# One VectorE operation for causal mask and row minimum of negated scores; gate columns beside the values; a new order of work

## The reference, cut to what matters

```python
h = _layernorm(x, axis=-1) * (1 + ca) + sa                 # ca, sa: one row per batch
# attention on h: RMS norm, then 16 heads of 64
sim = einsum('bhid,bhjd->bhij', q, k) * SCALE
sim = where(causal_mask, -finfo.max, sim)                  # mask above the diagonal
attn = softmax(sim, axis=-1)
out = einsum('bhij,bhjd->bhid', attn, v)
gates = sigmoid(x @ Wg)                                    # one gate per token and head
out = (gates * out) @ Wout
x = x + ga * out
h = _layernorm(x, axis=-1) * (1 + cb) + sb
# feed forward on h: silu(h Wg + bg) * (h Wu + bu) @ Wd + bd, plus experts:
sim = einsum('btphn,hkpn->pbthk', q, keys)                 # 2 x 4 heads x 64 keys
sc, ix = top_k(sim, 8)                                     # per half; then the best 8 of the 64 sums
x = x + gb * (mlp + experts)
```

## Time and profile before

| | us |
|---|---|
| median of three runs | 1555.74 (1555.52 to 1555.81) |
| the profiled execution, its own time | 1555.38 |
| its span in the trace | 1553.6 |
| PE busy | 1480.7 |
| DVE busy | 1347.4 |
| ACT busy | 1142.6 |
| POOL busy | 1098.7 |

### The profile page before, as it was taken

The page is one execution under the profiler, slowest core; times in us unless marked ns, Lnnn a source line. Parts: engine busy times, 40 slices in busy tenths (PEclk is TensorE's granted clock), DMA queues, the critical chain, the costliest instruction groups (busy, mean ns, idle before and its releaser), DMA issues.

```text
span 1553.6 us, 39532 instructions
## 1 busy us (share of the span) xinstructions
PE 1480.7 (95%) x12385; PEld 1194.9 (77%) x12385; DVE 1347.4 (87%) x3993; ACT 1142.6 (74%) x3687; POOL 1098.7 (71%) x1203
## 2 busy tenths in 40 slices
PE   4899999999999999999999999999999999999963
PEld 2577888787888878788887878888787888878753
DVE  4579998989999998999999899999989999998874
ACT  2677777887777788777778877777887777788731
POOL 2027787777778777777877777787777778777677
PEclk7899999999999999999999999999999999999976
DMA  4000000000000000000000000000000000000000
GB/s 126 18 14 18 14 23 22 22 17 15 20 14 22 22 22 15 17 18 16 22 22 22 15 17 17 17 22 22 22 15 17 16 18 22 22 22 8 12 12 9
DMA packets 46126, 32.01 MB, mean 21 GB/s; under 512 B 5680, under 2 KB 41328, under 8 KB 45968
## 3 DMA queue, kind: packets, MB, share of 16 engines
q1 hardware_dynamic: 45856, 31.20, 7.2%
q10 hardware_dynamic: 240, 0.43, 0.1%
HBM read 27.31 MB, written 4.31 MB: 20 GB/s over the span
## 4 chain that ended last, share of the span: by engine, by line
PE 90%; DVE 5%; POOL 2%; ACT 2%; issue 1%; DMA 0%; POOLq 0%; ACTq 0%; DVEq 0%
PE pS L1029 11%; PE pW L964 11%; PE pW L965 10%; PE pW L966 10%; PE pW L1045 9%; PE pS L1018 7%; PE pS L1014 7%; PE pW L1069 6%; PE pW L1105 4%; PE pW L1108 4%; PE pS L1020 3%; PE pW L1049 3%; PE pS L1021 2%; PE pW L1097 2%; POOL fexp L421 1%; PE pW L978 1%
## 5 line engine op out<-in xcount | busy, mean ns | idle before, releaser
L529 ACT ACTIVATE pS<-pS,nmx 128x128 f32<-128x128 f32 (+1 forms) x1024 | 390.4, 426 | 33.5 <-DVE nmx L728 30.9
L421 POOL TENSOR_TENSOR fexp<-fexp,fsum 128x512 f32<-128x512 f32 x256 | 342.1, 1373 | 64.9 <-DVE fexp L864 64.9
L745 DVE TENSOR_TENSOR p_sb<-pS,coef 128x256 f32<-128x256 f32 (+1 forms) x512 | 261.7, 552 | 8.9
L412 POOL TENSOR_TENSOR fsum<-ex 128x512 f32<-128x512 f32 x256 | 258.3, 1047 | 0.0
L521 ACT COPY pT<-pS 128x768 f32<-128x768 f32 x256 | 212.5, 848 | 19.5 <-PE pS L1029 19.5
L1029 PE MATMUL pS<-ident,p_sb 128*128 128x128 f32 x1536 | 217.4, 278 | 8.5 <-DVE p_sb L745 8.4
L1029 PEld LDWEIGHTS pS<-ident,p_sb 128*128 128x128 f32 x1536 | 171.4, 141 | 28.5 <-issue 16.3
L864 DVE TENSOR_SCALAR fexp<-fsum,top,rz 128x512 f32<-128x512 f32 x256 | 192.1, 813 | 1.2
L727 DVE TENSOR_REDUCE nmx<-pS 128x2 f32<-128x256 f32 x256 | 108.3, 423 | 91.2 <-PE pS L1021 84.9
L529 ACT ACTIVATION_READ_ACCUMULATOR pS<-pS,nmx 128x1 f32 x1024 | 185.7, 181 | 0.0
L728 DVE TENSOR_REDUCE nmx<-pS 128x2 f32<-128x512 f32 x256 | 174.1, 680 | 0.0
(11 more groups left out here) (178 smaller groups left out, 3923.1 us busy)
## 6 DMA issues: line engine op xcount, KB each, us to landing
modB<-mods_dram SPq DMA_DIRECT2D x32, 256.0 KB, 3.2
x_in<-in_L_attn_tokens SPq DMA_DIRECT2D x32, 128.0 KB, 2.1
modA<-mods_dram SPq DMA_DIRECT2D x32, 128.0 KB, 3.1
x_res<-in_L_attn_tokens SPq DMA_DIRECT2D x32, 128.0 KB, 3.0
out<-yo SPq DMA_DIRECT2D x32, 128.0 KB, 1.9
modC<-mods_dram SPq DMA_DIRECT2D x32, 64.0 KB, 3.1
fsum<-in_L_attn_Wkv SPq DMA_DIRECT2D x1, 1024.0 KB, 6.7
fsum<-in_L_attn_Wq SPq DMA_DIRECT2D x1, 512.0 KB, 4.9
```

The source lines that it names most:

```text
L412: ins = nc.gpsimd.tensor_tensor(fsum[:, k, h], ex[:, k, h, 0:NX].unsqueeze(2).broadcast_to([P, NX, NK]), ex[:, k, RH + h, :].unsqueeze(1). ...
L421: ins = nc.gpsimd.tensor_tensor(fexp[:, k, h, :], fexp[:, k, h, :], fsum[:, k, h].rearrange("p i j -> p (i j)"), ALU.mult)
L529: ins = nc.scalar.activation(ps, ps, ACT.Exp, bias=nmx[:, p % 2, h, k:k + 1], accum_out=den(p)[:, h, k:k + 1])
L745: ins = nc.vector.tensor_tensor(p_sb[:, p % 2, :, cols_of(k)], pS[:, p % 2, :, cols_of(k)], coef[:, :, k:k + 1].broadcast_to([P, 2, (k + 1 ...
```

## The change

In `scores`, the four mask products go, and with them the bfloat16 identity and mask. In `row_max`, the two reductions become four `tensor_tensor_reduce` operations, one per head and token block: each adds a float32 mask from SBUF to the scores in PSUM, negates, writes the result back in place and accumulates the row's minimum, which an accumulator read behind each operation writes to `nmx`. The exponential gets the factor -1. A `nop` (`apart`) stands ahead of the four.

The 16 gate columns stand ahead of the values of the first four heads; a token block's values now come in three pieces (272, 384 and 384 columns) in place of two of 512 and the gate projection. ACT takes the tanh of the gates from the first piece.

The scale and shift of the second LayerNorm move from DVE to ACT, where they are one operation on the transposed rows (`modulate_h`), with scale and shift loaded as two columns (`col`, a new DMA per batch; the load `modB` shrinks from 256 to 128 KB). The eight largest similarities are found in `shift`, straight from PSUM, before the exponential; `sim_tops` and the reductions of L832 go, one subtraction (`top_d`) and one exponential on ACT (into `tops`) come. `finish` handles both token blocks at once. On POOL, `add_heads(0)` and `fold(0)` stand ahead of `weigh(1)`. The lists of calls of all engines are written in another order.

```diff
+GV = 2 * DI
+VCUT = (0, 4, 10, H)
+NV = len(VCUT) - 1
...
+LARGEST = 3e38
...
-        ident_bf = sb("ident_bf", [P, P], BF16)
-        mask = sb("mask", [P, P], BF16)
+        mask = sb("mask", [P, TB * P])
...
                 weigh(0)
+                add_heads(0)
+                fold(0)
+                rstd2()
                 weigh(1)
-                add_heads(0)
-                rstd2()
                 rstd1()
-                fold(0)
+                add_heads(1)
                 rms1()
-                add_heads(1)
                 fold(1)
                 if isinstance(i, int) and i == -1:
                     split_weights()
...
-                                ins = nc.scalar.activation(ps, ps, ACT.Exp, bias=nmx[:, p % 2, h, k:k + 1], accum_out=den(p)[:, h, k:k + 1])
+                                ins = nc.scalar.activation(ps, ps, ACT.Exp, bias=nmx[:, p % 2, h, k:k + 1], scale=-1.0, accum_out=den(p)[:, h, k:k + 1])
...
-                        k, half = divmod(n, 2)
-                        evacuate(v[:, k, half * BANK:(half + 1) * BANK], w.bank("V", n)[:, :], "V", n)
+                        k, c = divmod(n, NV)
+                        heads = slice(VCUT[c] * DH, VCUT[c + 1] * DH)
+                        w.wait_full("V", n)
+                        bank = w.bank("V", n)
+                        first = 0
+                        if c == 0:
+                            first = H
+                            if k == 0 and w.live(-1):
+                                act.wait_ge(S(coef_ready), at(coef_ready, i - 1, 1))
+                            nc.scalar.activation(g_th[:, k, :], bank[:, 0:H], ACT.Tanh, scale=0.5)
+                        w.release(nc.scalar.copy(v[:, k, heads], bank[:, first:first + heads.stop - heads.start]), "V", n)
...
-                                             ACT.Exp).then_inc(S(ex_ready), 1)
+                                             ACT.Exp)
+                        if k == TB - 1:
+                            act.wait_ge(S(top_d_ready), at(top_d_ready, f, 1))
+                            if w.live(-2):
+                                act.wait_ge(S(cand_ready), at(cand_ready, g, 1))
+                            nc.scalar.activation(tops[:, :, :, :].rearrange("p a h n -> p (a h n)"), top_d[:, :, :, :].rearrange("p a h n -> p (a h n)"),
+                                                 ACT.Exp).then_inc(S(tops_ready), 1)
...
+                def modulate_h():
+                    if w.has("hT"):
+                        w.wait_full("hT")
+                        act.wait_ge(S(col_loaded), at(col_loaded, f, 16))
+                        o = w.bank("hT")[:, 0:N]
+                        nc.scalar.activation(o, o, ACT.Identity, bias=col[:, 0:1], scale=col[:, 1:2]).then_inc(S(h2T_mod), 1)
...
-                        nc.vector.reduce_max(nmx[:, s % 2, :, 0], pS[:, s % 2, :, 0:P], AX_X, negate=True)
-                        nc.vector.reduce_max(nmx[:, s % 2, :, 1], pS[:, s % 2, :, P:SW], AX_X, negate=True).then_inc(S(max_ready), 1)
+                        apart()
+                        for h in range(2):
+                            for k in range(TB):
+                                ps = pS[:, s % 2, h, cols_of(k)]
+                                ins = nc.vector.tensor_tensor_reduce(out=ps, in0=ps, in1=mask[:, (1 - k) * P:2 * P], scale=-1.0, scalar=LARGEST,
+                                                                     op0=ALU.add, op1=ALU.min, accum_out=nmx[:, s % 2, h, k:k + 1])
+                        ins.then_inc(S(max_ready), 1)
...
-                        link(ins, head_chain, f)
-                        link(nc.vector.tensor_tensor(h2[:, :, :], h2[:, :, :], modB[:, 1:2, :].broadcast_to([P, TB, D]), ALU.mult), head_chain, f)
-                        nc.vector.tensor_tensor(h2[:, :, :], h2[:, :, :], modB[:, 0:1, :].broadcast_to([P, TB, D]), ALU.add).then_inc(S(h2_ready), 1)
+                        ins.then_inc(S(h2_ready), 1)
...
-                        sim = w.bank("sim", k)[:, :].rearrange("p (g n) -> p g n", n=NK)
-                        link(nc.vector.reduce_max(top1[:, k, :], sim, AX_X), head_chain, f)
-                        w.release(nc.vector.tensor_tensor(sh[:, k, :, :], sim, top1[:, k, :].unsqueeze(2).broadcast_to([P, 2 * RH, NK]),
-                                                          ALU.subtract), "sim", k)
+                        sim = w.bank("sim", k)[:, :].rearrange("p (a h n) -> p a h n", a=2, n=NK)
+                        heads = slice(k * RH, (k + 1) * RH)
+                        apart()
+                        for a in range(2):
+                            for h in range(RH):
+                                ins = nc.vector.max(top_s[:, a, k * RH + h, :], sim[:, a, h, :])
+                        link(ins, head_chain, f)
+                        w.release(nc.vector.tensor_tensor(sh[:, k].rearrange("p (a h) n -> p a h n", a=2), sim,
+                                                          top_s[:, :, heads, 0:1].broadcast_to([P, 2, RH, NK]), ALU.subtract), "sim", k)
                         if k == TB - 1:
+                            nc.vector.tensor_tensor(top_d[:, :, :, :], top_s[:, :, :, :], top_s[:, :, :, 0:1].broadcast_to([P, 2, TB * RH, TK]),
+                                                    ALU.subtract).then_inc(S(top_d_ready), 1)
                             done(head_chain)
-
-                def sim_tops(k):
-                    if w.live(-1):
-                        dve.wait_ge(S(ex_ready), at(ex_ready, f, k + 1))
-                        apart()
-                        for j in range(2 * RH):
-                            ins = nc.vector.max(tops[:, j // RH, k * RH + j % RH, :], ex[:, k, j, :])
-                        ins.then_inc(S(tops_ready), 1)
 
...
+                        o = w.bank("y")[:, 0:N].rearrange("p (k d) -> p k d", k=TB)
+                        nc.vector.tensor_tensor(o, o, modC[:, 0:1, :].broadcast_to([P, TB, D]), ALU.mult).then_inc(S(y_gated), 1)
+                        dve.wait_ge(S(y_gated), at(y_gated, g, 1))
+                        dve.wait_ge(S(x2g_ready), at(x2g_ready, g, 1))
+                        if w.live(-3):
+                            dve.wait_ge(S(out_stored), at(out_stored, g, 0))
+                        w.release(nc.vector.tensor_tensor(yo[:, :, :], o, x2g[:, :, :], ALU.add), "y")
...
                 thresholds()
+                row_max(0)
+                row_max(1)
                 choose(0, 0)
                 choose(0, 1)
+                normalise(0)
+                normalise(1)
+                gated_down(0)
+                bias_product(1)
+                gated_down(1)
+                gate_product(1)
                 choose(1, 0)
-                row_max(0)
+                bias_product(2)
+                gate_product(2)
+                row_max(2)
+                row_max(3)
                 choose(1, 1)
-                row_max(1)
-                gated_down(0)
-                normalise(0)
-                ln1_stats()
-                normalise(1)
                 ln2_stats()
-                bias_product(1)
-                gate_product(1)
-                row_max(2)
-                gated_down(1)
-                bias_product(2)
-                row_max(3)
-                gate_product(2)
                 normalise(2)
                 normalise(3)
+                ln1_stats()
+                ln2_modulate()
                 bias_product(3)
-                ln2_modulate()
                 gate_product(3)
                 row_max(4)
+                row_max(5)
                 low_part(h2T_high, h2T, "hT")
+                normalise(4)
+                normalise(5)
                 ln1_modulate()
                 shift(0)
-                row_max(5)
-                normalise(4)
                 shift(1)
-                normalise(5)
-                sim_tops(0)
-                sim_tops(1)
+                row_max(6)
+                row_max(7)
                 low_part(xT_high, xT, "xT")
-                row_max(6)
-                finish(0)
-                row_max(7)
                 normalise(6)
-                finish(1)
+                finish()
                 normalise(7)
...
-                        k, half = divmod(n, 2)
+                        k, c = divmod(n, NV)
+                        lo = GV + (H + VCUT[c] * DH if c else 0)
+                        hi = GV + H + VCUT[c + 1] * DH
                         w.wait_free("V", n)
-                        w.filled(mm3(w.bank("V", n)[:, :], cols(xT, k * P, (k + 1) * P),
-                                     cols(s_qkv, 2 * DI + half * BANK, 2 * DI + (half + 1) * BANK)), "V", n)
-
...
-                            mm(ps[:, h, 0:P], qk[r, p % 4, 0:P], qk[r, p % 4, N:N + P], start=True, stop=False, skip_group_check=True)
+                            mm(ps[:, h, 0:P], qk[r, p % 4, 0:P], qk[r, p % 4, N:N + P], start=True, stop=True, skip_group_check=True)
                         for h in range(2):
 
```

(9 more changed lines are left out.)

224 lines of the change are left out of this document (102 added, 122 removed), and 10 rows, old and new, of the table order.

## The result

The changed kernel takes 1575.01 us (1573.75 to 1575.8, four runs); the kernel before, run beside it, 1555.78 (1555.52 to 1556.16). The ratio is 1.0123, with a 95% interval of 1.0105 to 1.014: slower, outside the predicted range of 1470 to 1548.

What follows compares the result with a forecast made beforehand. PE, without slack, was taken to bound the kernel at 45.38 us a batch. Afterwards PE needs 42.6, DVE 42.5 + 0.6 = 43.1, plus 0.5 gives 43.6; 1555.4 - 53 = 1502 us, range 1470 to 1548.

Steps and rivals of the forecast that it cites:

- PE's 42.6 us: PE's need per batch after losing 2.2 us of mask products and 0.55 on gate and values, from 45.38.
- The row minimum at 1.13 us a pair: DVE's four fused operations in `row_max`: 1.13 us a pair against 0.93, adding 1.6 us a batch.
- the slower rival: Accumulator reads on PSUM do not hide, row minimum 1.74 us a pair, 1631 us; decides from 1.35 a pair; chance 0.12.
- What costs nothing: ACT's five added operations, POOL's new order and SP's loads were taken to add no time to a batch.
- 42.5: DVE's occupied time in us per batch after the change, before the waits added by the new order.
- DVE's 43.0: DVE's occupied time per batch in the kernel before: 45.38 less 2.4 us of waits.
- The 0.5 for meshing: Added us per batch for PE and DVE, both nearly full, waiting for each other.
- The 0.6 behind the exponentials: DVE's added waits per batch, in us, for ACT's exponentials around pairs 4 to 6 in the new order.
- Head and tail: The 135 us before and 113 after the steady stretch, taken as unchanged within 5 us.
- 43.6: The forecast time of a steady batch in us, 1.78 less than before.
- the bound by a little: Main forecast, chance 0.60: DVE slightly fuller than PE, 43.1 to 44.4 us a batch, 1487 to 1526 us.
- the turn-round of the score banks: Rival, chance 0.14: DVE, ACT and PE take turns at `pS`, four double rounds costing 0.4 us more each; middle 1540 us.

Runs made afterwards that it cites:

- choose_behind_gate: The changed kernel with `choose(1, 0)` moved behind `gate_product(2)`, still ahead of `row_max(2)`: 1534.7 us, ratio 0.9863 to the kernel before.
- narrow_gpsimd_after: The changed kernel with POOL's products and sums on 8 of 512 columns, all waits kept: 1503.0 us, ratio 0.9668 to the kernel before.

## Why the prediction was wrong

Step by step, per batch:

- **PE's 42.6 us** held: 42.95, the masks worth 2.0 and the gate columns 0.44.
- **The row minimum at 1.13 us a pair** was mis-sized: 1.24. The value taken for 256 elements was 0.35 and it is 0.38; the second short one takes 0.25, not 0.215. That is 0.9 a batch, and short of the 1.35 at which the slower rival would decide. Accumulator reads hide on PSUM too. The estimate of 1.30 by the Trainium skill's "VectorE: DVE Perf Modes" (section on the TRN2 errata) was nearer than mine: its 0.39 for 256 elements meets 0.38, its 0.26 for 128 is above 0.21 to 0.25.
- **"What costs nothing"** is the step that failed. It followed POOL's new order for what POOL waits for and for who waits for POOL's results. It left out which DVE operations lie beside POOL's. `h2` moved beside `weigh(1)`: 1.1 us more on DVE. With 0.9 for the minima this is the difference between 42.5 and the 44.4 found. The trace of before had the hold, in `choose` at 813 ns in the mean for 540 undisturbed, and the prediction carried it along inside DVE's 43.0. The Trainium skill states it in "SBUF — State Buffer", section "Who interferes with whom": a VectorE operation in a 2-port mode contends with GpSimd, and whoever issues first holds the shared pair for its whole instruction while the other is blocked; one with two SBUF inputs contends with a GpSimd instruction that reads SBUF. The trace agrees in both forms: up to 1318 ns with one tensor input, for 342 undisturbed, and up to 1359 with two.
- **The 0.5 for meshing** was far too small. It named this very wait, "PE ... at banks that DVE releases (the gated products, the output projection's)", and gave it no size. The walk that was missing goes from `project_out` back four places in `order` to `gate_product(2)`, and from there up DVE's list to `choose(1, 0)`. There stand 2.83 us of masks in place of 1.0, and 1.21 of them reach PE; the move of `choose_behind_gate` gives back 1.28.
- **The 0.6 behind the exponentials** held: 17.0 / 28.5 = 0.60.
- **Head and tail**, left as they were "within 5 us", cost 7.6 of the 19.5 us by which the span grew. The first output projection starts 7.7 us later (91.78 for 84.05). Between the first and the last lie 31 distances, 1415.2 us for 1400.0; the steady 0.385 each accounts for 11.9 of these 15.2, and the other 3.2 are the net of the first and the last ones (the very first is 47.5 for 41.7). From the start of the last one to the end it is 3.4 shorter (66.1 for 69.5), although that projection takes 6.61 us behind a wait of PE of 4.84, at a granted clock of 0.52 between 1507 and 1513 us, and 3.84 at the full level in the kernel before.

From 43.6 to 45.77, 1.27 is the bank's release (45.77 to 44.50); 0.32 is the hold on `h2` (44.50 to 44.18). The last 0.58, from 43.6 to 44.18, was not split by a run, and its cause stays open. It is not DVE's sum: in `narrow_gpsimd_after` DVE waits 2.7 us a batch and is occupied for 41.5 of 44.18, PE for 42.7. PE has waits there for `p_sb`, `aoT` and `pT`, some 1.5 us a batch, as in every variant of the new order that has the mask on DVE; the dearer minima may lengthen them. So DVE as "the bound by a little", the mechanism of the forecast, did not come either. Of the rivals, the turn-round of the score banks predicted the kind of loss, two nearly full engines passing waits to each other, at another bank. The slower rival had the right sign by a mechanism that did not come.

## What to carry to other kernels

When a change leaves no engine full, walk every PSUM bank back to the call that frees it, and count what stands ahead of that call in its engine's list, at the durations it has beside its new neighbours. A DVE operation of a form that POOL holds (here `TENSOR_SCALAR` within SBUF, and `SCALAR_TENSOR_TENSOR` with two SBUF inputs) costs what is left of POOL's running operation besides its own time; put it beside POOL's idle stretches, and never ahead of a release that a nearly full engine needs. The sign in a profile is one form with a wide spread of durations and no wait beside it. A relief for the full engine is worth having only with its order: the same arithmetic gave 1575 us and, with one call moved past two others, 1535.

## What the runs showed of the hardware

- A DVE `TENSOR_SCALAR` within SBUF waits for POOL's running `TENSOR_TENSOR`: 128 elements take up to 1318 ns for 342, and 512 up to 1490 ns for the 540 of the idle case (2.83 and 1.00 us for two from start to end). The two-input form on SBUF takes up to 1359 ns. Operations that read PSUM keep their times: the minimum's 0.29 at 734.05 with POOL at work from 733.07 to 734.40. So do the row statistics from SBUF: 274 to 285 ns, also at 742.48 with POOL at work.
- The fused operation with accumulator costs 0.21 to 0.25 us for 128 and 0.38 for 256 elements in PSUM, with the mask from SBUF. Its accumulator read lasts 0.14 us instead of the 0.08 behind an SBUF operation, and is hidden behind the next operation but for about 0.04 us in these rows (0.25 where the read of an operation on 256 elements precedes, 0.21 where none does).
